# Mixing one pair's second half in a single burst of eight key tiles instead of two bursts of four

## The reference

```python
q, k, v = einsum('bsx,xMnd->Mbnsd', x, qkv)            # 16 heads of 64
a = einsum('bnsd,bntd->bnst', q, k) * 64 ** -0.5
bias = where(rel >= 0, cumsum(rpe_bias)[clip(rel)], -30000.0)   # causal, by distance
mix = einsum('bnst,bntd->bnsd', softmax(a + bias), v)
x = layernorm(x + einsum('bnsd,ndx->bsx', mix, out_w))
r = sigmoid(shift_mix(x, mu_r) @ W_r.T); k = relu(shift_mix(x, mu_k) @ W_k.T) ** 2
x = layernorm(x + r * (k @ W_v.T))
```

## Time and profile before

| | |
|---|---|
| median of three runs | 1304.31 us |
| profiled execution, own time | 1305.56 us |
| span of its trace | 1303.8 us |
| PE busy | 1120.3 us, 86% |
| POOL busy | 886.4 us, 68% |
| DVE busy | 842.9 us, 65% |
| ACT busy | 743.1 us, 57% |
| granted TensorE clock, mean | 0.968 |

### The profile page before, as it was taken

How to read it: one execution, slowest core, us unless ns; L and a number is a source line. 1 busy time by engine, 2 the same in 40 slices (tenths; PEclk the granted TensorE clock), 3 DMA queues, 4 the chain that set the end, 5 groups by cost and what they waited for, 6 DMA issues and landing times.

```text
span 1303.8 us, 21982 instructions
## 1 busy us (share of the span) xinstructions
PE 1120.3 (86%) x6909; PEld 782.4 (60%) x6909; DVE 842.9 (65%) x2505; ACT 743.1 (57%) x1857; POOL 886.4 (68%) x527
## 2 busy tenths in 40 slices
PE   5424999999999999999999999999999999999985
PEld 3313666666666666666666666666666666666664
DVE  1411666666666676777776767767667777676756
ACT  2312666666666565665665656656556665565632
POOL 1432878777777677877666777776677777666740
PEclk9666999999999999999999999999999999999997
DMA  5776555555554555665545556554554665544710
GB/s 144 167 85 147 132 132 131 128 118 124 142 121 123 128 136 132 152 147 117 140 120 134 130 142 151 135 123 119 139 142 122 150 152 132 117 119 123 207 45 19
DMA packets 104353, 168.38 MB, mean 129 GB/s; under 512 B 10656, under 2 KB 66352, under 8 KB 104240
## 3 DMA queue, kind: packets, MB, share of 16 engines
q1 hardware_dynamic: 104240, 166.98, 53.6%
HBM read 41.63 MB, written 24.64 MB: 51 GB/s over the span
## 4 chain that ended last, share of the span: by engine, by line
PE 62%; DVE 16%; issue 8%; DMA 6%; ACT 6%; SPq 2%; DVEq 0%; POOL 0%; ACTq 0%
PE ps_o L933 20%; PE ps_t L917 15%; PE ps_rows L903 12%; PE ps_m L878 6%; DMA bias_by_distance<-x_t 6%; DVE prob L613 4%; DVE pt L630 4%; PE ps_m L947 3%; PE ps_m L883 3%; ACT pt L480 2%; DVE mix_sb L636 2%; DVE k_lo L599 1%; ACT prob L469 1%; DVE q_lo L599 1%; DVE shift L680 1%
## 5 line engine op out<-in xcount | busy, mean ns | idle before, releaser
L421 POOL TENSOR_SCALAR prob<-prob,inv 128x128 f32<-128x128 f32 (+7 forms) x512 | 879.2, 1728 | 369.5 <-DVE inv L620 367.4
L469 ACT ACTIVATE prob<-prob,low 128x128 f32<-128x128 f32 (+7 forms) x512 | 395.2, 773 | 140.7 <-DVE low L613 138.4
L613 DVE CUSTOM_DVE_ANT_0 prob<-ps_rows,table 128x128 f32<-128x128 f32 (+7 forms) x512 | 383.3, 749 | 134.8 <-PE ps_rows L903 106.4
L903 PE MATMUL ps_rows<-stacks 128*128 128x512 f32 (+3 forms) x1536 | 403.7, 373 | 64.4 <-DMA stacks<-k_lo 41.7
L917 PE MATMUL ps_t<-ident,prob 128*128 128x128 f32 x2304 | 349.9, 279 | 86.4 <-ACT pt L480 49.1
L917 PEld LDWEIGHTS ps_t<-ident,prob 128*128 128x128 f32 x2304 | 261.0, 141 | 198.2 <-issue 130.9
L903 PEld LDWEIGHTS ps_rows<-stacks 128*128 128x128 f32 x1536 | 247.2, 191 | 83.0 <-DMA stacks<-k_lo 41.9
L630 DVE COPY pt<-ps_t 128x256 f32<-128x256 f32 (+2 forms) x320 | 178.9, 567 | 180.5 <-PE ps_t L917 179.4
L480 ACT ACTIVATE pt<-ps_t 128x128 f32<-128x128 f32 (+2 forms) x448 | 203.3, 476 | 152.1 <-PE ps_t L917 152.0
L933 PE MATMUL ps_o<-pt,v_pair 128*64 128x512 f32 (+3 forms) x1536 | 268.6, 492 | 0.0
L933 PEld LDWEIGHTS ps_o<-pt,v_pair 128*64 128x64 f32 x1536 | 101.8, 136 | 181.8 <-issue 172.3
(11 more groups left out here) (106 smaller groups left out, 561.4 us busy)
## 6 DMA issues: line engine op xcount, KB each, us to landing
stacks<-k_hi SPq DMA_DIRECT2D x124, 256.0 KB, 4.9
stacks<-k_lo SPq DMA_DIRECT2D x124, 256.0 KB, 4.9
stacks<-q_hi SPq DMA_DIRECT2D x62, 256.0 KB, 4.5
stacks<-q_lo SPq DMA_DIRECT2D x62, 256.0 KB, 4.8
mix_transposed<-mix_sb SPq DMA_DIRECT2D x62, 256.0 KB, 2.0
table<-bias_by_distance SPq DMA_DIRECT2D x64, 192.0 KB, 2.6
mix_tile<-mix_transposed SPq DMA_DIRECT2D x24, 512.0 KB, 5.0
w_cur<-in_L_attn_qkv SPq DMA_DIRECT2D x32, 192.0 KB, 3.3
```

The lines of the kernel that those rows point to most:

```text
L421: nc.gpsimd.tensor_scalar(row, row, inv[:, r:r + 1], None, ALU.mult).then_inc(s_norm, 1)
L469: nc.scalar.activation(row, row, ACT.Exp, bias=low[:, r:r + 1], scale=-1.0, accum_out=total[:, r:r + 1]).then_inc(s_exp, 1)
L613: nc.vector.tensor_tensor_reduce(prob[:, r % PSLOTS, 0:width], ps_rows[:, score_at(r):score_at(r) + width], table[n % 2][:, h, SEQ - width ...
L903: ins = nc.tensor.matmul(ps_rows[:, at + c0:at + c1], q_st(h, n)[:, P * i:P * i + P], k_st(h, n, low_part)[:, c0:c1], start=(low_part == 0 ...
```

## The change

The far half's two bursts become one. Slot 2 holds no mix any more, slot 5 neither; slot 4 issues all eight key tiles behind the `x1` transpose and ahead of row 4's transposes. DVE's copy of `ps_o` moves from slot 6 to slot 5. The number and shape of the instructions are the same.

```diff
-MIX_FAR = (2, 5)
+MIX_FAR = 4
...
-                    if prev and slot == MIX_FAR[1] + 1:
+                    if prev and slot == MIX_FAR + 1:
                         store_mix(n - 1, 1)
...
-                    if prev and slot in MIX_FAR:
-                        at = GROUP * MIX_FAR.index(slot)
-                        mix(n - 1, 1, at, at + GROUP)
+                    if prev and slot == MIX_FAR:
+                        mix(n - 1, 1, 0, TILES)
```

## The result

The changed kernel takes **1371.05 us** (median of four runs, 1363.7 to 1377.46); the kernel before, on the same chip in four runs, 1305.08 (1304.12 to 1306.07). The ratio is **1.0504, interval 1.0441 to 1.0567**: 66 us slower. The forecast had the sign, but its 1352 is 19 us short; its own range ended at 1358, that with the rivals at 1361. The profiled execution took 1375.33, with a span of 1373.6; the forecast's sum was +47.9 on 1303.8, the measured one is +69.8.

The account below looks back on a forecast made before the run. PE's instruction list at 2.4 GHz was taken as the bound; 22 tiled pairs by 1.66, 8 plain by 1.33 and 0.8 for the last pair gave +47.9 us on 1304.31, so 1352 us; own range 1345 to 1358, with rivals 1334 to 1361.

Parts of the forecast that it names:

- Step 1: Slots 2 to 4: projection 1, without the first burst, newly waits for `q_lo`, 1.11 us tiled, 0.79 plain.
- Step 2: Slot 4: merged burst takes 5.72 us plus 0.1 entry; PE itself is +0.95 us a tiled pair, +0.63 plain.
- Rival (d): Tiling switches: only their saving counts, `q_lo` ready without a wait, 0.25 us a pair won, 1297 us; chance 0.02.
- Step 3: Slots 5 to 8: DVE and ACT work queues behind the burst, delaying row 9's transposes 1.66 us tiled, 1.33 plain.
- row 8's fifth tile: Before row 9's transposes: PE's wait there for ACT's evacuation ends ahead and adds nothing to the 1.66 us.
- Rival (a): Behind `k_hi`: DVE and ACT take the delay up, only PE's own shift stays, 26.4 us, 1331 us; chance 0.12.
- so the next pair starts like this one: Slot 11: DVE and ACT both wait for PE again, each over 1 us, so no further delay carries over.
- What costs nothing: SyncE's transfers, row 8's exponential and POOL, +1.92 us but ending row 15 at 735.2, wanted at 736.7.
- rival (b): Bias 10 or POOL's gapless stretch: the whole 1.92 us stays in a tiled pair, 56.9 us, 1361 us; chance 0.07.
- POOL as waker of a transpose: In the next profile, PE's transposes released by POOL: named as one sign that the forecast is wrong.
- clock still 1.00: In the next profile, PE's granted clock stays at its higher level, 2.4 GHz.
- last pair: The pair with no projection: only the `x1` chain is uncovered, taken as 0.8 us (bounds 0 and 1.9).

Follow-up runs that it names:

- e2: Changed kernel, but with two bursts of four tiles in slots 4 and 5 and the copy of `ps_o` back in slot 6; 1345.02 us, ratio 1.0303.
- e6: Changed kernel, but projection 0 is written to the bank `ps_o`, so projection 1 need not wait for `q_lo`; 1345.81 us, ratio 1.0303.
- e3: Changed kernel, merged burst still in slot 4, but with DVE's copy of `ps_o` back in slot 6; 1350.45 us, ratio 1.0338.
- e9: Kernel before, with DVE's copy of the mix in slot 9 and SyncE's store of it between the two `stack_k`; 1302.13 us, ratio 0.9967.
- e4: Changed kernel, with row 13's score and row 8's first four tile transposes issued twice in the eight plain pairs; 1364.19 us, ratio 1.0442.
- e1: Changed kernel, but with the whole merged burst in slot 2 and the copy of `ps_o` in slot 3; 1335.43 us, ratio 1.0235.
- e5: Changed kernel, but with two bursts of four tiles in slots 2 and 4, the copy staying in slot 5; 1336.76 us, ratio 1.0242.
- e8: Kernel before, with DVE's copy of the mix in slot 9 and SyncE's store of it behind both `stack_k`; 1306.54 us, ratio 1.001.

## Why the prediction was right, and where it was wrong

**Step 1, the wait for `q_lo`: right.** 1.10 us measured for 1.11, and in the plain pair projection 1 stands at 265.51 (315.42 less that pair's 49.91) as worked out. e2 has the same wait with two bursts, e6 takes it away by another bank.

**Step 2, the burst: nearly right.** Its way to the next transposes is 5.74 us for 5.72. With the entry, from the `x1` transpose to projection 2, the added time is 5.90 where 5.82 was taken. What the merged switches save depends a little on where one reads it: 3.68 + 2.40 - 5.83 = 0.25 us a pair to the next transposes, 3.57 + 2.45 - 5.90 = 0.12 to the next projection. (The Trainium skill's rule in TensorEngine Tiling (Array Packing), Key Properties, that a change of tiling mode drains TensorE, agrees in direction.) The saving does not reach the end: e3, with one burst, is 0.10 us a pair slower than e2, with two. Rival (d), 1297, is out.

**Step 3, what is late next: right in its chain, a little short in size.** Bias 10 at 717.18 for 717.01, exponential 11 +1.81 for +1.66, reciprocal, evacuation of row 8, row 9's transposes at 722.49 for 722.34. 0.08 us is the burst and its entry above, 0.10 the chain from a projection that has waited to the `x1` transpose (2.54 us for 2.44); of the two together 0.15 arrives at row 9. A wait of 0.78 us before row 8's fifth tile, which I had set aside as ending ahead, does end ahead in tiled pairs, as I had argued. Rival (a), that DVE and ACT take the delay up, fell: DVE's 0.44 us were all they had. That the place of `store_mix` is a term of its own is shown by e3, 0.51 us tiled and 0.33 plain.

**Behind row 9: POOL's delay, priced at nothing, costs 0.20 us.** The forecast ended at row 9's transposes, "so the next pair starts like this one", and under "What costs nothing" it let POOL come 1.92 us later, because POOL's last row still had 1.5 us of slack. From row 10 on POOL is 2.00 us later in the pair, while PE and DVE are only 1.80 later. The instruction that feels it is DVE's L680 in slot 13. DVE and POOL there, first in the kernel before:

```profile
731.12 0.63 DVE L680 TENSOR_TENSOR shift<-y,x 128x128 f32<-128x128 f32 x1
...
730.49 2.84 POOL L421 TENSOR_SCALAR prob<-prob,inv 128x1024 f32<-128x1024 f32 x1
```

and in the kernel after, where L680 stands at 813.11 with 0.82 us (above):

```profile
810.19 2.52 POOL L421 TENSOR_SCALAR prob<-prob,inv 128x896 f32<-128x896 f32 x1
812.69 2.84 POOL L421 TENSOR_SCALAR prob<-prob,inv 128x1024 f32<-128x1024 f32 x1
```

L680 starts 0.63 us behind the start of POOL's row 15 in one and 0.42 behind it in the other, and ends 1.25 us behind it in both. So it ends 0.20 us later against the rest of the pair, ACT's L490 waits 1.41 us for 1.21, and PE's wait in slot 14 is 0.88 for 0.68. That is 0.20 us a tiled pair. In e3, with the copy back in slot 6, POOL is only as late as the others, L680 is back at 0.63 us and PE's wait in slot 14 at 0.69. With this term a tiled pair is 2.0 us longer, near rival (b)'s 1.92, and POOL has a part in it, though not by a transpose that waits for POOL. This is the second step that failed, beside the clock below.

**POOL as waker of a transpose: my sign of a wrong forecast, and it seemed to come.** The profile puts the wait of 0.97 us in slot 13 down to POOL instead of ACT. But the transposes there are row 13's, and `transpose` (L909) waits for that row, which POOL had finished by 810.2, 2.5 us before. What ends at 812.71 is POOL's row 14, by chance together with ACT's evacuation (812.73). The wait is for ACT, as in the kernel before, where the same evacuation ends at 730.73 and the transposes start at 730.71. In e9, the fastest, POOL is named 24 times. So who is named as ending a wait says little when its length stands and two engines end together.

**The failing step: "clock still 1.00".** The sum multiplied delays of pairs at one clock. It holds in tiled pairs. In plain ones PE's idle time in slots 8 and 9, where there is no tile work between, is followed by a fall to 1.2 GHz in all eight pairs of the traced execution, and 1.58 us go in each. e4 shows that it is these idle places: filling them brings the level and the 1.58 us back with everything else as it was; e3, with shorter waits there, has no fall either. But the waits make a fall possible, not certain: e1, e5 and e6 have them at the same length, and four, two and two of their eight plain pairs fall. What decides between these pairs is not shown. The spread of the changed kernel's runs fits with a varying number of falls (mean clocks of 0.957 to 0.966 in spans of 1375.7 to 1362.0), but only one of them was traced.

The account of the miss, in us:

```
                        forecast           measured
tiled pairs (22)        22 x 1.66 = 36.5   22 x 2.01 = 44.2   +7.7: 0.15 to row 9, 0.20 behind it
plain pairs (8)          8 x 1.33 = 10.6    8 x 1.47 = 11.8   +1.1
fall of the clock        0                  8 x 1.58 = 12.6  +12.6
last pair                0.8                1.2               +0.4
sum                     47.9               69.8              +21.9
```

This is the traced execution, with eight falls; it ran 4.3 us above the kernel's median. By the medians the change costs 66.0 us and e4, without the falls, is 6.9 us faster than the changed kernel. So in the traced execution the clock is the largest step that failed; by the medians it weighs about as much as the terms of the tiled pair, 7.7 us together.

By parts of the change, tiled and plain: moving the first burst to slot 4 costs 1.40 and 1.05 (e2), merging the second into it 0.10 and 0.10 (e3), the copy in slot 5 0.51 and 0.33 (e3 beside the changed kernel; the 0.20 through POOL is within the 0.51), the clock 0 and 1.58. Terms of this kind don't stand for themselves in any order, though: e1 loses 0.65 to 0.84 a pair by leaving slot 5, which in e2 is not left.

**What stays open.** It is not settled what holds L680, which has two SBUF inputs of 128x128, beside POOL. In the last pair, without POOL work beside it, it takes 0.29 us. In all eleven traces one that starts 0.4 to 0.65 us behind the start of a POOL instruction ends 1.25 to 1.27 behind it, and one that starts 1.3 us or more behind it takes 0.29 again. (The Trainium skill, SBUF — State Buffer, Who interferes with whom, says that a DVE instruction with two SBUF inputs contends with a GpSimd instruction that reads SBUF. The longer times beside POOL agree.) It is not held for the whole of POOL's 2.84 us. No experiment here moved POOL alone, so the cause is only argued. L673 of e8 is open as well: 0.22 us in the kernels before and after (as L672), 1.09 in e8.

## What to carry to other kernels

Work on an engine that does nothing for its neighbours may still be their cover: before moving it, list what the other engines finish behind it (here `q_lo` in slot 2, `k_lo`, an evacuation and a bias in slot 5), since a merged burst gives one cover where there were two. Price a copy in an in-order queue by what it stands ahead of; moving it three slots later was the only gain found here. "Slack" of an engine counts only for those that wait for it: POOL had it, and its delay still lengthened an instruction of DVE. And when a forecast adds idle time to TensorE, sum it over neighbouring places and ask what the clock will do there, pair type by pair type.

## What the runs showed of the hardware

The clock fell although PE never idled for a whole microsecond: two idle times of 0.79 and 0.98 us, 1 us apart, were followed by 3.4 us at 1.2 GHz. In tiled pairs, which have 0.78 and 0.54 us at the same places, it did not fall, nor in the plain pairs of the kernel before, with one wait of 1.22 us there. Nor is it sure to come behind such waits: with 0.78 and 0.99 us it came in eight, four, two and two of eight pairs in the changed kernel, e1, e5 and e6. A fall can therefore come from waits that each look harmless, and adding PE work there (e4) made the kernel 6.9 us faster by the medians. A mean clock over a slice hides it: 0.96 over 310 us was all that the coarse table showed, and the windows of 1 us were needed to see it.
